# Five edits to the borders of a macaron block: loads on one queue, another search for the widest weight, tile 1 normalised on ScalarE, another order in the first two tiles, and the last mixer tile in other PSUM banks

## What is computed

```python
x = x + 0.5 * ffn(layernorm(x))
x = x + mixer(layernorm(x))
x = x + 0.5 * ffn(layernorm(x))

# ffn(x): a second layernorm with gamma and beta inside
y = silu(h @ w1 + b1)                 # w1 = (q1 - 128) * scales, one scale per 128 rows
return x + 0.5 * (y @ w2 + b2)        # w2 = (q2 - 128) * scales
# mixer(x)
a = sigmoid(x @ Wa + ba); b = x @ Wb + bb; c = tanh(x @ Wc + bc)
s[t] = a[t] * s[t-1] + (1 - a[t]) * b[t]
return (c * s) @ Wy + by + x @ Wd + bd
```

## Time and profile before

| | |
|---|---|
| median of 3 runs | 776.76 us (774.44 to 776.85) |
| the profiled execution's own time | 776.82 us |
| its span, first to last instruction | 775.0 us |
| TensorE / ScalarE / GpSimd / VectorE busy | 95% / 85% / 83% / 83% |
| from 60 to 90 us: TensorE / GpSimd busy | 30.00 / 28.00 of 30 us |

### The profile page before, as it was taken

How to read it: one execution, slowest core, us unless ns; L and a number is a source line. 1 busy time by engine, 2 the same in 40 slices (tenths; PEclk the granted TensorE clock), 3 DMA queues, 4 the chain that set the end, 5 groups by cost and what they waited for, 6 DMA issues and landing times.

```text
span 775.0 us, 13958 instructions
## 1 busy us (share of the span) xinstructions
PE 733.0 (95%) x3234; PEld 547.0 (71%) x3234; DVE 641.7 (83%) x1244; ACT 659.0 (85%) x1113; POOL 644.0 (83%) x829
## 2 busy tenths in 40 slices
PE   1689999999999999989999997999999999999996
PEld 0467777777777776757877875677777777777774
DVE  3498898999999999668887783888999999999886
ACT  4579999999999998768888887999899999999984
POOL 5789999999999997748666685999999999999753
PEclk9999999999999999999999997999999999999999
DMA  8720000000000000000000000000000100000001
GB/s 265 239 86 0 2 0 0 1 0 0 0 0 0 1 1 1 1 0 2 0 0 0 1 0 2 0 29 28 28 27 33 48 28 27 27 28 28 28 28 57
DMA packets 19846, 20.24 MB, mean 26 GB/s; under 512 B 1574, under 2 KB 19420, under 8 KB 19804
## 3 DMA queue, kind: packets, MB, share of 16 engines
q1 hardware_dynamic: 18396, 17.66, 7.1%
q10 hardware_dynamic: 1312, 2.10, 0.8%
q0 software_dynamic: 96, 0.00, 0.0%
HBM read 11.37 MB, written 8.39 MB: 25 GB/s over the span
## 4 chain that ended last, share of the span: by engine, by line
PE 87%; issue 3%; DVE 3%; ACT 3%; POOL 2%; DMA 2%; DVEq 0%; ACTq 0%; POOLq 0%
PE ps_fc L808 30%; PE ps_z L808 27%; PE ps_z L838 13%; PE ps_fc L903 6%; PE ps_tr L801 4%; PE ps_tr L854 3%; PE ps_fc L911 2%; DMA q_int<-in_L_ffn_fc_q 2%; PE ps_fc L897 1%; DVE z_acc L641 1%; PE ps_z L801 1%; POOL rstd L351 0%; ACT g_native L523 0%; POOL cs_parts L413 0%; DVE stats L613 0%
## 5 line engine op out<-in xcount | busy, mean ns | idle before, releaser
L641 DVE SCALAR_TENSOR_TENSOR z_acc<-ps_z,cols,z_acc 128x512 f32<-128x512 f32 x384 | 276.5, 742 | 19.1 <-PE ps_z L808 17.2
L394 POOL TENSOR_TENSOR g_lo<-g_full,g_hi 128x512 fp32r<-128x512 f32 x192 | 248.6, 1295 | 44.3 <-ACT g_hi L528 40.7
L506 ACT ACTIVATE u_sb<-ps_fc,cols 128x512 f32<-128x512 f32 x256 | 199.7, 780 | 62.7 <-PE ps_fc L808 56.4
L630 DVE SCALAR_TENSOR_TENSOR y_sb<-ps_fc,cols,u_sb 128x512 f32<-128x512 f32 x256 | 190.2, 743 | 61.3 <-ACT u_sb L506 61.1
L808 PE MATMUL ps_fc<-h_hi,q_sb 128*128 128x512 f32 x512 | 229.5, 448 | 7.8 <-DVE y_sb L630 2.6
L808 PE MATMUL ps_fc<-h_lo,q_sb 128*128 128x512 f32 x512 | 203.8, 398 | 0.0
L808 PE MATMUL ps_z<-g_hi,q_sb 128*128 128x512 f32 x384 | 154.2, 401 | 1.4 <-DVE z_acc L641 1.0
L808 PE MATMUL ps_z<-g_lo,q_sb 128*128 128x512 f32 x384 | 151.5, 395 | 0.0
L526 ACT ACTIVATE g_full<-y_sb 128x512 f32<-128x512 f32 x192 | 120.0, 625 | 3.6 <-DVE y_sb L630 3.6
L808 PEld LDWEIGHTS ps_fc<-h_hi,q_sb 128*128 128x128 f32 x512 | 98.2, 192 | 35.0 <-issue 10.1
L838 PE MATMUL ps_z<-g_native,w_full 128*128 128x512 f32 x256 | 120.2, 591 | 0.0
(11 more groups left out here) (91 smaller groups left out, 974.3 us busy)
## 6 DMA issues: line engine op xcount, KB each, us to landing
resid<-in_L_attn_x SPq DMA_DIRECT2D x16, 512.0 KB, 4.3
out_x<-resid SPq DMA_DIRECT2D x16, 512.0 KB, 2.9
q_int<-in_L_ffn_fc_q ACTq DMA_DIRECT2D x2, 1024.0 KB, 9.6
z_acc<-in_L_ffn_fc_scales SPq DMA_DIRECT2D x1, 256.0 KB, 7.2
wd_sb<-in_L_attn_Wd SPq DMA_DIRECT2D x1, 256.0 KB
resid<-in_L_attn_Wy SPq DMA_DIRECT2D x2, 64.0 KB
wab_sb<-in_L_attn_Wa SPq DMA_DIRECT2D x1, 64.0 KB
wab_sb<-in_L_attn_Wb SPq DMA_DIRECT2D x1, 64.0 KB
```

What stands on the lines that cost most here:

```text
L394: nc.gpsimd.tensor_tensor(g_lo[:, slot, :], g_full[:, g % 2, :], g_hi[:, slot, :].bitcast(F32), ALU.subtract).then_inc(g_ready, 1)
L506: nc.scalar.activation(u_sb[:, f % 2, :], ps_fc1[:, f % 2, 0, :], ACT.Identity, bias=col(R_B1 + f), scale=col(R_S1 + f)).then_inc(u_ready, 1)
L630: nc.vector.scalar_tensor_tensor(out=y_sb[:, f % 4, :], in0=ps_fc1[:, f % 2, 1, :], scalar=col(R_S1 + FC + f), in1=u_sb[:, f % 2, :], op0= ...
L641: nc.vector.scalar_tensor_tensor(out=z, in0=bank_of(g, n, par), scalar=col(R_S2 + KC * g + n), in1=z, op0=ALU.mult, op1=ALU.add).then_inc( ...
```

## The change

**Loads.** SP issues x of tile 0 in two halves, then q1 in two, q2 in two, the scales, x of tiles 1, 2 and 3, and then the mixer's weights. ScalarE issues the nine small `rows` loads (six were SP's, three GpSimd's). `bias_raw`, `wy_raw` and `wc_raw` get tensors of their own, so x needs no wait for the mixer's weights.
**Search.** VectorE looks through the integers, in four pieces as they land; the conversions on ScalarE come later (`convert_q1`, and q2 after the prologue's `affine`).
**Tile 1.** In both feed-forward stages its `normalise` runs on ScalarE at f == 2 of tile 0, and its `rsqrt` stands on GpSimd at f == 0 of tile 0. The last mixer tile has neither any more. Half of tile 0's `normalise` goes to ScalarE too. The product that makes `w2_full` moves from GpSimd to VectorE.
**Order.** The five step constants get a value for `before` 0, 1 and 2. The third one is the old one. In tile 0 the `rsqrt` of tile 2 stands at f == 5 (before 2), its `normalise` at 6 and 7 (5 and 6), the turns of tile 1 at 4 and 5 (0 and 2), ScalarE's `affine` of tile 1 at 5 and 6 (1 to 3), both `h_low` at 4 (3 and 4). In tile 1 these are 3, 6 and 7, 2 and 4, 3 to 5, and 5 and 6. `statistics(2)` and its `variance` move from f == 1 to f == 3 of tile 0.
**Mixer.** Rounding its weights goes to ScalarE (tile 13), GpSimd (tile 14) and VectorE (tile 15). In mixer tile 0 `c_sum` comes ahead of the scan. The last mixer tile's output goes to `ps_z`; its `y_products` and `add_mixer` come at f == 1, and the wait for them stands before fc2 at f == 4.
**Ends.** The last tile is stored in two halves; 14 products on `ident` (`warm_up`) stand at TensorE's start.

```diff
-    RSQRT_AT = 2
...
+    RSQRT_AT = (5, 3, 2)
...
+    LOWER_PART_AT = ((4, 4), (5, 6), (3, 4))
...
+    WARM_UP = 14
...
+            if type(t) is int and t == NT - 1:
+                return ps_z[:, half, :]
+            return ps_mix[:, par, half, :]
...
+            sp.dma_start(resid[:, 0, 0:2, :], x_view[:, 0, 0:2, :]).then_inc(x_half_loaded, 16)
+            sp.dma_start(resid[:, 0, 2:4, :], x_view[:, 0, 2:4, :]).then_inc(x_loaded[0], 16)
+            for k in range(KC):
+                sp.dma_start(q1_int[:, k, :], q1[k * P:(k + 1) * P, :]).then_inc(q1_loaded[k], 16)
+            q2_view = q2.rearrange("(g p) d -> p g d", p=P)
+            for k, part in enumerate(q2_halves):
+                sp.dma_start(q2_int[:, part, :], q2_view[:, part, :]).then_inc(q2_loaded[k], 16)
...
+            for par in range(2):
+                sp.wait_ge(x_loaded[par], 16)
+                sp.dma_start(resid[:, 2 + par, :, :], x_view[:, 2 + par, :, :]).then_inc(x_loaded[par], 16)
...
-            sp.wait_ge(mixer_ready, 1)
...
+            with sp.Fori(0, NT - 1) as t:
...
+            for half in range(2):
+                blocks = slice(2 * half, 2 * half + 2)
+                sp.wait_ge(ffn_added, 4 * NT - 1 + half)
+                sp.dma_start(out_view[:, NT - 1, blocks, :], resid[:, NT - 1, blocks, :]).then_inc(stored, 16)
...
+                    lower_at, normalise_at = LOWER_PART_AT[before], NORMALISE_AT[before]
                     for f in range(FC):
                         if f >= 1:
                             g_low(ff, f - 1, par)
                         elif before:
                             g_low(ff - 1, FC - 1, 1 - par)
-                        if f in LOWER_PART_AT:
-                            if behind >= 1:
-                                h_low(ln + 1, ff + 1, 1 - par, LOWER_PART_AT.index(f))
-                            elif ff0 == 0:
-                                xn_low(0, 0, LOWER_PART_AT.index(f))
+                        else:
+                            rsqrt(ln0 + 1, True)
+                        for c in range(KC):
+                            if f == lower_at[c] and behind >= 1:
+                                h_low(ln + 1, ff + 1, 1 - par, c)
+                            elif f == lower_at[c] and ff0 == 0:
+                                xn_low(0, 0, c)
                         if behind >= 2 or ff0 == 0:
                             t2, twice = (t + 2, True) if behind >= 2 else (1 - behind, False)
-                            if f == RSQRT_AT:
+                            if f == RSQRT_AT[before]:
                                 rsqrt(ln + 2, twice)
-                            if f in NORMALISE_AT:
-                                normalise(ln + 2, t2, halves[NORMALISE_AT.index(f)])
+                            if f in normalise_at:
+                                normalise(ln + 2, t2, halves[normalise_at.index(f)])
                         if behind >= 1 and f == RESIDUAL_AT:
                             residual(ln + 1, t + 1)
+                        if ff0 == 0 and behind == 1 and f == 7:
+                            prepare_mixer()
                 if ff0 == 0:
                     rsqrt(ln0, True)
-                    normalise(ln0, 0)
+                    normalise(ln0, 0, halves[0])
                     residual(ln0, 0)
                     for c in range(KC):
                         h_low(ln0, ff0, 0, c)
-                    rsqrt(ln0 + 1, True)
-                    normalise(ln0 + 1, 1)
-                    pool.wait_ge(s2_loaded, 16)
-                    pool.wait_ge(w2_int_ready, 1)
-                    nc.gpsimd.tensor_tensor(w2_full[:, :, :], w2_full[:, :, :], s2_wide,
-                                            ALU.mult).then_inc(w2_ready, 1)
...
-                rsqrt(t + (NT + 2), twice)
+                if behind:
+                    rsqrt(t + (NT + 2), behind == 1)
...
+            act.wait_ge(rows_zero, 1)
...
+            for src, r, n in small:
+                act.dma_start(rows[r:r + n, :], src).then_inc(rows_loaded, 16)
+            for v, r, at in ((ba, R_AB, 0), (bb, R_AB, N), (bc, R_C, N)):
+                act.dma_start(rows[r:r + 1, at:at + N], v.rearrange("(a n) -> a n", a=1)).then_inc(rows_loaded, 16)
...
+            def convert_q1(k):
+                act.wait_ge(q1_loaded[k], 16)
+                nc.scalar.activation(q1_sb[:, k, :], q1_int[:, k, :], ACT.Copy,
+                                     bias=-ZERO_POINT).then_inc(q1_ready, 1)
...
+            def normalise(ln, t, blocks, signal):
+                act.wait_ge(shift_ready, ln + 1)
+                wait(act, turned, 2 * ln)
+                for a in blocks:
+                    last = nc.scalar.activation(xhat[:, a, :], resid[:, t, a, :], ACT.Identity,
+                                                bias=shift[:, 0, a:a + 1], scale=rstd[:, 0, a:a + 1])
+                last.then_inc(signal, 1)
...
+                act.wait_ge(mixer_loaded, 16 * 10)
+                nc.scalar.activation(wc_parts[:, :, 0, :], wc_raw[:, :, :], ACT.Copy)
+                nc.scalar.activation(wy_hi[:, :], wy_raw[:, :], ACT.Copy)
+                nc.scalar.activation(bias_parts[:, :, :], bias_raw[:, :, :], ACT.Copy).then_inc(mixer_rounded, 1)
...
+                        if not before and f == 2:
+                            normalise(ln0 + 1, 1, range(SUB), xhat_ready)
+                        if ff0 == 0 and behind == 2 and f == 7:
+                            round_mixer()
                 if ff0 == 0:
+                    normalise(ln0, 0, halves[1], xhat_half_ready)
+                    convert_q1(0)
                     for c in range(KC):
                         affine(ln0, ff0, 0, c, bank=(ps_tr, ps_tr2)[c])
+                    convert_q1(1)
+                    for k in range(KC):
+                        act.wait_ge(q2_loaded[k], 16)
                     nc.scalar.activation(w2_full[:, :, :], q2_int[:, 0:NATIVE, :], ACT.Copy,
                                          bias=-ZERO_POINT).then_inc(w2_int_ready, 1)
+                    nc.scalar.activation(q2_sb[:, :, :], q2_int[:, NATIVE:FC, :], ACT.Copy,
+                                         bias=-ZERO_POINT).then_inc(q2_ready, 1)
...
-                        if ff0 and not before and f == 0:
+                        if ff0 and not before and f == 1:
                             for half in range(2):
                                 add_mixer(NT - 1, 1, half)
-                        if ff0 == 0 and not before and f == 3:
-                            prepare_mixer()
-                        if not before and f == 1:
+                        if ff0 == 0 and not behind and f == STATISTICS_AT[0]:
+                            lower_bias()
+                        if not before and f == 3:
                             if ff0 == 0:
                                 dve.wait_ge(x_loaded[0], 32)
...
-                    statistics(0)
+                    statistics(0, halves[1])
                     variance(ln0)
-                    largest_of(0, q1_sb, q1_ready, 1)
-                    largest_of(1, q2_sb, q2_ready, 1)
+                    for k in range(KC):
+                        largest_of(k, q1_int[:, k, :], q1_loaded[k])
+                    for k, part in enumerate(q2_halves):
+                        largest_of(KC + k, q2_int[:, part, :].rearrange("p g d -> p (g d)"), q2_loaded[k])
                     find_width()
                     dve.wait_ge(x_loaded[1], 16)
                     statistics(1)
                     variance(ln0 + 1)
+                    dve.wait_ge(s2_loaded, 16)
+                    dve.wait_ge(w2_int_ready, 1)
+                    nc.vector.tensor_tensor(w2_full[:, :, :], w2_full[:, :, :], s2_wide,
+                                            ALU.mult).then_inc(w2_ready, 1)
...
+            def largest_of(i, q, loaded):
+                dve.wait_ge(loaded, 16)
+                nc.vector.tensor_reduce(out=largest[:, i:i + 1], in_=q, axis=AX.X, op=ALU.max,
+                                        apply_absolute_value=True).then_inc(largest_found, 1)
...
-                scan(t, par)
+                if before:
+                    scan(t, par)
                 dve.wait_ge(c_part_ready, t + 1)
                 nc.vector.tensor_tensor(c_sum, ps_c[0:N, :], c_part, ALU.add).then_inc(c_sum_ready, 1)
+                if not before:
+                    scan(t, par)
...
+            warm_up()
+            pe.wait_ge(rows_loaded, 16 * 9)
...
+                        if ff0 and not before and f == LAG:
+                            pe.wait_ge(mix_added, 2 * NT)
...
-                        if ff0 and not before and f == 0:
+                            turn(ln + 1, TURN_AT[before].index(f))
+                        if ff0 and not before and f == 1:
                             y_products(NT - 1, 1)
-                            pe.wait_ge(mix_added, 2 * NT)
...
+                    if before == 2 and not behind:
```

(1 more changed line is left out.)

159 lines of the change are left out of this document (73 added, 86 removed).

## The result

The changed kernel took 779.92 us (median of 5 runs, 778.86 to 781.74), the kernel before 776.26 us (774.44 to 776.85, 5 runs). The ratio is 1.0054, with a 95% interval of 1.0041 to 1.0068: slower by about half a per cent. Forecast were 778.1, inside a range of 772.8 to 781.2, with 0.28 for slower by over 0.3%, which is what came, and 0.47 for no change.

The account below looks back on a forecast made before the run. TensorE, 95% busy, was taken to lose time at five stops, with GpSimd's list a second bound. From the profiled 776.82: -0.6 - 1.6 + 0.2 + 3.8 - 0.5 = +1.3, so 778.1 us, range 772.8 to 781.2.

Parts of the forecast that it names:

- my case: Whole kernel: the time lands between 776.4 and 780.0 us, around the sum of 778.1; chance 0.46.
- S: Start of the first feed-forward's first product: 16.2 us, kept within 15.5 to 17.0, against 20.50 before.
- The new wait: Tile 0: late rsqrt holds VectorE at tile 3's variance; TensorE goes on at S + 24.5, after 5.7 us.
- The low clock: Behind TensorE's stop in tile 0: five microseconds of work at half speed.
- rival 1: Clock stays at 2.4 GHz through tile 0's stop, or VectorE isn't held: each border 2.5 shorter, 773.1; chance 0.24.
- Its other condition: Alternative within rival 1: VectorE isn't held in tile 0, each border also 2.5 us shorter; within the same 0.24.
- S + 50.1 to the turn of tile 3: First feed-forward: TensorE turns tile 3 50.1 us after the first product starts, at 66.3 against 66.93: 0.6 less.
- The border to the second feed-forward: Mixer's end through tile 0: earlier start, same wait, tile 3 turned at 513.6 against 509.75: 3.8 us more.
- the prediction's own sign: Check in the trace: tile 3 turned 48 us after the first product of the second feed-forward.
- Rival 3: GpSimd's list is no bound, early starts are kept, tile 0's two waits go: 761 us; chance 0.05.
- Mixer start, rounding, store: Mixer tile 0 order 1.6 us less; rounding weights in tiles 13 to 15 0.2 more; halved last store 0.5 less.

Follow-up runs that it names:

- the second trace: Profile of the changed kernel run once more, unchanged: median 780.72 us (1.0052 of the kernel before), profiled execution 780.73 us.
- The two single moves: The changed kernel with tile 2's rsqrt ahead of both h_lo in tile 0: 769.89 us; separately, with tile 3's variance after step 7 there: 775.21 us.
- the undone edits: The changed kernel with the scan first in mixer tile 0, the last tile stored in one piece and no warm-up products: 783.57 us.

## Why the forecast was right, and where it was wrong

The working gave 778.1, the runs 779.9, inside my case (776.4 to 780.0, 0.46) but at its upper end, and slower where no change had the larger chance. The mechanism was right, one term was too small, and the first feed-forward came out right in the first trace partly by luck.

- **First product.** Forecast S = 16.2 (15.5 to 17.0); 15.60 in the first trace, 16.48 in the second, 15.8 to 17.3 in those of the experiments that issue the small loads on ScalarE. The last small load, issued at 3.94 (4.14 and 4.31 in two of them), is down at 8.6 to 10.2, so a queue of its own did not free it from the traffic beside it; on SyncE's queue, ahead of the weights, it was down by 6.45. The Trainium skill, "DMA: Bandwidth & Descriptors", section "Queues, rings and completion order", says that the DMA engines take turns between the queues, packet by packet. The first trace agrees in so far as that load overtook both halves of q2: these were issued from 2.69 on, and the search of them begins at 10.25. The first product at 15.5 that came of it was nearly met in one trace of ten (15.60). The warm-up products, which the prediction ended before 5 us, ran until 6.87, 1.7 ahead of the product on `rows` in the first trace, so nothing waited for them there.
- **The new wait.** Forecast: VectorE held about 8 us, TensorE stopped from S + 18.8 to S + 24.5. Trace: 8.39 us, S + 18.0 to S + 23.5, and the same in the second feed-forward. The two single moves showed that the late rsqrt is the cause, worth 10 us; VectorE's hold alone is 4.7 of them.
- **The low clock.** Taken were five microseconds at half speed; the trace has about 4, and keeping TensorE busy gave back 1.4 to 1.9 a border. That run is the case of rival 1, the clock at 2.4 GHz through the stop: it put the first `g_lo` of tile 1 at S + 33.7, and there it is at S + 33.5 (49.31, first product 15.82). Its price of 2.5 a border was too high because the case it was compared with had this `g_lo` at S + 36.2 and the trace has S + 34.9. Its other condition, VectorE not held, was given the same price; with the variance moved it gave back 2.1 and 2.8.
- **S + 50.1 to the turn of tile 3.** Measured 50.15, by errors that cancel. u of step 2 came at S + 5.0, not 5.8, since already the third fc1, from 19.33 on, had products 0.23 to 0.34 us apart, where the first two had 0.43. The first `g_lo` of tile 1 came at S + 34.9, not 36.2; but from that `g_lo` to the turn it took 15.25, not 13.9. I had counted GpSimd's list there as without a gap, and it has 1.18 of waiting for a `g_hi` (59.66). Its work alone takes 13.9, as counted. In the second trace less cancels: M1 is 50.7.
- **The border to the second feed-forward, the term that was too small.** Its start was right: the first product at 465.3 in the time of the kernel before (462.43 + 2.88, forecast 465.4), u of step 2 at 469.5 (469.3), the rsqrt 16.6 behind it (16.7). (The prediction's times for the last `cs_parts` add up to 467.15, not 467.05, which changes nothing.) From the rsqrt to the turn of tile 3 it took 29.2, forecast 27.6: the same gap in GpSimd's list, here 1.30, and little to cancel it. That is nearly all of what lies between +3.8 and +5.55, and tile 3 was turned 50.0 us behind the first product, where the prediction's own sign said 48. The step that failed is the one from the first `g_lo` of tile 1 on, seven subtractions (8.7), an rsqrt (3.0) and a whole normalise (2.2), read as the only bound. What makes the gap was not separated: with tile 1's steps earlier TensorE's waits are gone and M1 and M2 are shorter, yet GpSimd still waits 1.43 for a `g_hi`, at another place of its list.
- **Rival 3**, 761 us, needed a shorter list on GpSimd. 760.9 was reached without a shorter list, in another order.
- **Mixer start, rounding, store**: -1.8, +0.1, -0.75 for -1.6, +0.2, -0.5; the undone edits confirm the first, and a gain from the store between 0.3 and 0.8.
- **Medians.** The difference of the two traces, 2.0, is 1.7 less than that of the medians, since an execution of the change varies by up to 2.9 us. I had given S a spread of 1.5 and the rest of the path none from one execution to the next; the second trace shows both, 0.88 in S and 1.0 behind it.

## What to carry over

When a step is moved behind others on one engine, look for who waits not for its result but for leave to overwrite its inputs: here a guard against overwriting held VectorE for 8 us, and what was queued behind it stopped TensorE. Put small steps that others wait for into the idle time ahead of the bulk work, even where their own result is not needed yet. Moving one half normalise out of such idle time cost 3.0 us. And an engine's list of work is a lower bound: where its entries wait for another engine's, the sum of their durations is too short.

## What was not expected of the hardware

Filling a 5.4 us stop in each feed-forward with 24 products that nobody reads left the granted clock behind it at 1.00 instead of 0.50 and made the kernel 3.4 us faster. The same waits of 0.98 and 1.13 us in the two feed-forwards of one execution were followed by 0.75 in the first and by 1.00 in the second. The same order with the same waits of 1.58 and 1.42 us was granted 1.00 in the kernel before and 0.66 over 341 to 346 in the run with the edits undone. Nine small loads on a queue of their own, the last one issued at 3.94 to 4.31, were down at 8.6 to 10.2 beside the large ones, but by 6.45 on the queue of the large ones and ahead of q1, with the last issued at 4.47.
